# A transformer layer on one core: attention's weighted values issued four steps at a time, with two score banks and four maximum banks

## The chip, the cores and the metric

The kernel runs on one core of a Trainium2 chip. The metric is the time of one launch on the device in microseconds (us); the median of three runs is compared. The engines of the core are TensorE (PE, with its weight loads listed apart as PEld), VectorE (DVE), ScalarE (ACT), GpSimd (POOL) and SyncE (SP), which here only issues DMAs. They run side by side, each through its own list of instructions in order, and wait for one another on semaphores.

## What is computed

A layer with modulated layer norms: attention, then a feed-forward stage. The change lies in the attention, which is, for 4 sequences of 2048 tokens, 512 channels and 16 heads of 32:

```python
k = (c_kv @ W_k_up).reshape(Bb, Tt, NH, HD)
v = (c_kv @ W_v_up).reshape(Bb, Tt, NH, HD)
q = (x @ W_q).reshape(Bb, Tt, NH, HD)
scores = jnp.einsum('bqhd,bkhd->bhqk', q, k)
scores = scores + jnp.einsum('bqr,bkr->bqk', q_rope, k_rope)[:, None]
scores = jnp.where(causal[None, None], -jnp.inf, scores / scale)
w = jax.nn.softmax(scores, axis=-1)
attn = jnp.einsum('bhqk,bkhd->bqhd', w, v).reshape(Bb, Tt, D_MODEL)
```

All is in float32. Projections before it and the feed-forward stage behind it are not touched.

## The kernel before

Three stages follow one another: `projection`, `attention`, `feedforward`. The attention works in 16 **units** u (4 sequences by 4 groups of `GH` = 4 heads). A unit has 4 chunks j of 512 queries. Chunk j needs 4(j+1) **steps** i, each a block of 128 keys against the chunk's queries; a unit has 40 steps s, chunk 0 the steps 0 to 3, chunk 1 the steps 4 to 11, chunk 2 the steps 12 to 23 and chunk 3 the steps 24 to 39. The last four steps of a chunk are on the diagonal, and only 512, 384, 256 and 128 queries wide (`step_width`).

- **Scores** (`scores`, lines 1206 and 1207): for each of the four heads of a step two matmuls into one bank of PSUM, out of `SBANKS` = 3 that are used in turn. ScalarE takes the exponential of a head (line 1046) into a buffer of probabilities, `RING` = 5 of them. The first matmul of a head waits until ScalarE is through with the head that used the bank before (`probs_ready`, at + 1).
- **Weighted values** (`weighted_values`, lines 1213 and 1231): probabilities times values into the bank `ps_o`, 32 output columns for each head. They come `LAG` = 2 steps late and two steps at a time, in a **part** behind the scores of every odd step (`over_two_steps`).
- **Denominators**: the sums over keys. `SHARE_OF` gives each step an owner. Probabilities of a step "G" are added up by POOL (lines 1143 and 1146), those of a step "T" go through TensorE against ones into the bank `ps_d`. `close_denominators` (line 1245) puts POOL's sum into `ps_d` once for each chunk, in the part that takes the chunk's last steps. VectorE then inverts `ps_d` in four instructions (line 1095) and multiplies (line 1099); the list `extras` puts these among the maxima of the two steps behind the part.
- **Maxima** (`maximum`, line 1190): the row maxima that the exponentials subtract are worked out ahead for the next unit, in 160 **pieces** a unit (one matmul each, into one of `MBANKS` = 3 banks), reduced by VectorE (line 1082 for whole blocks, 1085 for those on the diagonal, whose widths are 128 to 512). `deal` spreads the pieces over the steps by a price list: `streams(m)` is TensorE's time in a pair of steps, `closes(m)` what VectorE's closing work takes from the pair at `FIRST[j] + 2`, the steps 2, 6, 14 and 26. TensorE issues pieces between the heads of a step and behind its part (the loop at line 1264).
- **Low queries**: `q_b`, `QB_RING` = 3 buffers, loaded by SP (`load_q_b`) in the order written in `body`; a row of each takes the negated maxima (`place_max`).

The loop that sets TensorE's order:

```python
for t in range(NU * NSTEP + LAG):
    parts = [lambda hh=hh: scores(*STEP_OF[t], hh) for hh in range(GH) if t < NU * NSTEP]
    closing = CLOSE_AT.get(t)
    if t > LAG and t % 2 == 1:
        parts.append(lambda: over_two_steps(t, closing))
    items = PLAN.get(t, [])
    for n, part in enumerate(parts):
        part()
        for it in items[len(items) * n // len(parts):len(items) * (n + 1) // len(parts)]:
            maximum(it)
```

## Time and profile before

| what | value |
|---|---|
| median of 3 runs | 3611.91 us (3610.14 to 3612.38) |
| the profiled execution | 3614.76 us, its span 3613.0 us |
| granted TensorE clock, mean | 0.990 |
| TensorE matmuls busy | 3506.1 us (97%) |
| VectorE busy | 2540.1 us (70%) |
| GpSimd busy | 2673.6 us (74%) |
| ScalarE busy | 1811.9 us (50%) |

A share is busy time over the whole span. A matmul's end is modelled and matmuls overlap, so a share of 97% does not say that each moment did work: how far TensorE runs at its pace is read from the distance between the starts of its rows.

### The profile page before, as it was taken

The numbers are of one execution on the slowest core, as the hardware profiler recorded it, in microseconds if no ns is written. First come the engines' busy times: TensorE is split into PE (matmuls) and PEld (weight loads), VectorE is DVE, ScalarE is ACT, GpSimd is POOL, SyncE is SP. The second block draws the span as 40 slices with busy tenths as digits, with TensorE's granted clock in tenths as the row PEclk, the third lists the DMA queues.
The fourth block names the chain that finished last, engine by engine and source line by source line (L and its number), as shares of the span: only waits on it lengthen the run. The fifth ranks groups of instructions, "written<-read, shape, count | busy, mean of one in ns | idle before, by whom it ended". The sixth has DMA issues, their size and how long they took to land. (4 is left out here: it accounts for less than half of the span.)

```text
span 3613.0 us, 54217 instructions
## 1 busy us (share of the span) xinstructions
PE 3506.1 (97%) x19552; PEld 2408.8 (67%) x19552; DVE 2540.1 (70%) x5329; ACT 1811.9 (50%) x3455; POOL 2673.6 (74%) x1194
## 2 busy tenths in 40 slices
PE   8999989999999999999999999999999699999999
PEld 4777756666666666666666666666665488888887
DVE  6676777777777777677777777777775366666665
ACT  2434335555555555555555555555555344444443
POOL 2333349889898898898988989889889566666665
PEclk9999989999999999999999999999999799999999
DMA  5778763463534535436346353463552111212120
GB/s 197 272 273 304 260 169 72 108 140 78 132 87 110 138 79 117 113 90 146 80 100 147 74 131 92 102 138 83 114 125 72 62 59 70 70 70 71 70 70 36
DMA packets 232756, 426.58 MB, mean 118 GB/s; under 512 B 25380, under 2 KB 26916, under 8 KB 232488
## 3 DMA queue, kind: packets, MB, share of 16 engines
q1 hardware_dynamic: 232424, 423.10, 43.2%
q8 instruction: 155, 2.54, 0.3%
q14 instruction: 113, 0.93, 0.1%
q10 hardware_dynamic: 64, 0.02, 0.0%
HBM read 300.86 MB, written 121.65 MB: 117 GB/s over the span
## 5 line engine op out<-in xcount | busy, mean ns | idle before, releaser
L1046 ACT ACTIVATE att_probs<-att_ps_s 128x512 f32<-128x512 f32 (+3 forms) x2560 | 1301.7, 536 | 938.7 <-PE att_ps_s L1207 850.1
L1146 POOL TENSOR_TENSOR att_sum_g<-att_sum_g,att_probs 128x2048 f32<-128x2048 f32 (+3 forms) x400 | 1626.0, 4065 | 72.8 <-ACT att_probs L1046 34.0
L1082 DVE TENSOR_REDUCE att_piece_max<-att_ps_m 128x1 f32<-128x512 f32 x1520 | 945.5, 681 | 136.1 <-PE att_ps_m L1190 134.2
L1206 PE MATMUL att_ps_s<-att_q_a,att_k_a 128*128 128x512 f32 (+3 forms) x2560 | 952.0, 374 | 17.2 <-DMA att_q_b<-att_neg_max 7.0
L1207 PE MATMUL att_ps_s<-att_q_b,att_k_b 65*128 65x512 f32 (+3 forms) x2560 | 934.6, 367 | 0.0
L1085 DVE CUSTOM_DVE_ANT_0 att_ps_m<-att_ps_m,mask_qk 128x128 f32<-128x128 f32 x1008 | 477.6, 508 | 268.2 <-PE att_ps_m L1190 254.9
L1190 PE MATMUL att_ps_m<-att_k_a,att_q_a 128*128 128x512 f32 (+3 forms) x1808 | 650.6, 384 | 5.9 <-DVE att_piece_max L1085 3.6
L1206 PEld LDWEIGHTS att_ps_s<-att_q_a,att_k_a 128*128 128x128 f32 x2560 | 486.1, 190 | 129.6 <-ACT att_probs L1046 42.5
L1213 PE MATMUL att_ps_o<-att_probs,att_v 128*32 128x512 f32 (+3 forms) x5120 | 546.8, 536 | 4.2 <-POOL att_probs L1126 4.2
L1207 PEld LDWEIGHTS att_ps_s<-att_q_b,att_k_b 65*128 65x128 f32 x2560 | 484.8, 189 | 65.7
L1190 PEld LDWEIGHTS att_ps_m<-att_k_a,att_q_a 128*128 128x128 f32 x1808 | 341.2, 190 | 225.0 <-issue 76.2
L1095 DVE RECIPROCAL att_ps_d<-att_ps_d 128x128 f32<-128x128 f32 x256 | 235.3, 943 | 156.4 <-PE att_ps_d L1213 156.4
L1143 POOL TENSOR_TENSOR att_sum_g<-att_probs 128x1536 f32<-128x1536 f32 (+1 forms) x64 | 275.8, 4310 | 87.1 <-ACT att_probs L1046 85.8
L1213 PEld LDWEIGHTS att_ps_o<-att_probs,att_v 128*32 128x32 f32 x5120 | 139.0, 109 | 279.9 <-issue 204.9
L1126 POOL TENSOR_SCALAR_AFFINE_SELECT att_probs<-att_probs 128x512 f32<-128x512 f32 x256 | 160.5, 640 | 142.0 <-ACT att_probs L1046 141.8
L1190 PE MATMUL att_ps_m<-att_k_next,att_q_a 128*128 128x128 f32 (+1 forms) x720 | 255.6, 388 | 0.0
L1190 PEld LDWEIGHTS att_ps_m<-att_k_next,att_q_a 128*128 128x128 f32 x720 | 131.4, 189 | 87.8 <-DVE att_piece_max L1082 27.4
L513 POOL TENSOR_TENSOR prj_h_lo<-prj_h_f,prj_h_hi 128x512 fp32r<-128x512 f32 x64 | 84.2, 1342 | 112.4 <-ACT prj_h_hi L450 112.4
L1401 DVE TENSOR_TENSOR ffn_x<-ffn_ps_ffn,ffn_gate 128x512 f32<-128x512 f32 x64 | 44.2, 691 | 173.2 <-PE ffn_ps_ffn L62 173.2
L1562 ACT ACTIVATE ffn_act_f<-ffn_relu 128x512 f32<-128x512 f32 x64 | 40.5, 633 | 248.7 <-DVE ffn_relu L1474 248.6
L1085 DVE DVE_READ_ACCUMULATOR2_ANT att_piece_max<- 128x1 f32 x1008 | 143.5, 142 | 0.0
L1537 ACT CAST att_q_a<-ffn_ps_t 128x512 fp32r<-128x512 f32 x128 | 75.2, 588 | 128.5 <-DVE ffn_ps_t L1442 127.5
(189 smaller groups left out, 4955.8 us busy)
## 6 DMA issues: line engine op xcount, KB each, us to landing
att_q_a<-s_q_hi SPq DMA_DIRECT2D x128, 256.0 KB, 5.9
att_q_a<-s_qr_hi SPq DMA_DIRECT2D x128, 256.0 KB, 6.7
prj_x_sb<-in_x_dram SPq DMA_DIRECT2D x16, 1024.0 KB, 5.2
s_q_hi<-prj_q_hi SPq DMA_DIRECT2D x16, 1024.0 KB, 4.2
s_q_lo<-prj_q_lo SPq DMA_DIRECT2D x16, 1024.0 KB, 6.0
s_k_hi<-prj_k_hi SPq DMA_DIRECT2D x16, 1024.0 KB, 4.5
s_k_lo<-prj_k_lo SPq DMA_DIRECT2D x16, 1024.0 KB, 6.4
s_v<-prj_v_sb SPq DMA_DIRECT2D x16, 1024.0 KB, 9.1
```

The source lines that it names most:

```text
L513: pool.tensor_tensor(h[1][:, c, :], h_f[:, c, :], as_f32(h[0][:, c, :]), ALU.subtract).then_inc(hlo_ready, 1)
L1046: act.activation(probs[t % RING][:, hh, c0:CH], ps_s[(GH * t + hh) % SBANKS][:, c0:CH], ACT.Exp, scale=SCALE).then_inc(probs_ready, 1)
L1082: dve.tensor_reduce(top, ps_m[:, bank, :], AX_X, ALU.max).then_inc(piece_taken, 1)
L1085: dve.tensor_tensor_reduce(ps_m[:, bank, 0:width], ps_m[:, bank, 0:width], keep["mask_qk"][:, CH - width:CH], 1.0, MASKED, ALU.add, ALU.ma ...
L1095: dve.reciprocal(cols, cols).then_inc(rden_ready, 1)
L1126: pool.affine_select(out=at, in_=at, compare_op=ALU.is_ge, fill=0.0, base=0, pattern=[[0, GH], [1, P]], channel_multiplier=-1).then_inc(cl ...
L1143: pool.tensor_tensor(sum_g[:, :, c0:CH], first[:, :, c0:CH], new, ALU.add).then_inc(sum_added, 1)
L1146: pool.tensor_tensor(sum_g[:, :, c0:CH], sum_g[:, :, c0:CH], new, ALU.add).then_inc(sum_added, 1)
L1190: mm(ps_m[:, bank, 0:width], q_a[j][:, hh, r * P:(r + 1) * P], keys, start=True, stop=True).then_inc(piece_ready, 1)
L1206: mm(out[:, c0:CH], k_a[:, hh, i * P:(i + 1) * P], q_a[j][:, hh, c0:CH], start=True, stop=False)
L1207: last = mm(out[:, c0:CH], k_b[:, hh, i * P:(i + 1) * P], q_b[low_queries(u, j)][0:2 * HD + 1, hh, c0:CH], start=False, stop=True)
L1213: last = mm(out[hh * HD:(hh + 1) * HD, c0:CH], stat(hh), mov[:, hh, c0:CH], start=start, stop=stop, skip_group_check=True)
```

## The change

Eight edits, all in the attention. The weighted values of four steps go in one part, behind every fourth step (`TOGETHER` = 4), not of two behind every second. The closings of chunks 1 and 2 come one part later, four steps on (`CLOSE_LATER`), and in every part the closing stands behind the values; the copy of `ps_o` by ScalarE stays where it was (`TAKE_AT`). There are six probability buffers, not five, two buffers of low queries, not three, two score banks, not three, and four maximum banks, not three. SP loads the low queries later and in another order. `deal` counts the values of four steps at the pair that holds them, at most `VALUES_MOST` = 9 for a pair, and shifts pieces by up to a step; its `closes` still names the steps 2, 6, 14 and 26.

```diff
-RING = 5
-QB_RING = 3
-SBANKS = 3
-MBANKS = 3
+RING = 6
+TOGETHER = 4
+QB_RING = 2
+SBANKS = 2
+MBANKS = 4
...
-ENDS_ON_PE = [owners[-1] == "T" for owners in SHARE_OF]
-OPENED_BY_SUM = ["T" not in owners.rstrip("T") for owners in SHARE_OF]
+CLOSE_LATER = (0, 4, 4, 0)
+OPENED_BY_SUM = ["T" not in owners for owners in SHARE_OF]
...
-    due = [(2 * m - 2) % NSTEP, (2 * m - 1) % NSTEP]
+    due = [(2 * m - n) % NSTEP for n in range(1, TOGETHER + 1)] if 2 * m % TOGETHER == 0 else []
...
-    return own / CH + GH * any(FIRST[j] == (2 * m) % NSTEP for j in range(TCH))
+    return (own + min(values, VALUES_MOST * CH)) / CH
+VALUES_MOST = 9
 PIECE, CLOSING = 2.8, 19
...
-            out[2 * m + half] = items[done:round(seen)]
+            some = items[done:round(seen)]
+            for n, it in enumerate(some):
+                at = 2 * m + half + (n + 0.5) / len(some) - 2 * pairs[0]
+                out.setdefault(2 * pairs[0] + int(at * pace), []).append(it)
...
-        CLOSE_AT = {NSTEP * u + FIRST[j] + STEPS[j] - 1 + LAG: (u, j) for u in range(NU) for j in range(TCH)}
+        TAKE_AT = {NSTEP * u + FIRST[j] + STEPS[j] - 1 + LAG: (u, j) for u in range(NU) for j in range(TCH)}
+        CLOSE_AT = {t + CLOSE_LATER[j]: (u, j) for t, (u, j) in TAKE_AT.items()}
...
                     wait_alone(sp, scores_ready, GH * (NSTEP * u + NSTEP), sp_mark)
                     place_max(u + 1, 1)
+                    load_q_b(u + 1, 1)
                     load_k_a(u + 1, TCH - 1)
                     load_q_a(u + 1, TCH - 1)
-                    load_q_b(u + 1, 2)
                     load_k_b(u + 1, TCH - 1)
...
-            def over_two_steps(t, closing):
-
-                if closing and ENDS_ON_PE[closing[1]]:
-                    close_denominators(*closing)
-                for due in (t - LAG - 1, t - LAG):
+            def over_four_steps(t, closing):
+
+                for due in range(t - LAG - TOGETHER + 1, t - LAG + 1):
                     weighted_values(*STEP_OF[due])
-                if closing and not ENDS_ON_PE[closing[1]]:
+                if closing:
                     close_denominators(*closing)
...
-                if t > LAG and t % 2 == 1:
-                    parts.append(lambda: over_two_steps(t, closing))
+                if t > LAG and (t - LAG) % TOGETHER == TOGETHER - 1:
+                    parts.append(lambda: over_four_steps(t, closing))
```

How many pieces stand in each step of a middle unit follows from `maximum_plan`, steps 0 to 39 (turns of a finished set of maxima are counted with them):

```
before 6 0 0 6 6 1 1 5 5 3 3 5 6 0 1 5 6 5 6 5 5 1 0 6 5 1 0 6 6 6 5 7 6 6 5 5 6 4 4 5
now    7 3 0 4 6 3 1 4 7 3 1 5 7 2 0 6 6 5 5 6 6 1 0 0 7 6 0 1 7 7 5 4 7 6 4 6 6 5 2 3
```

TensorE's instructions from the start of step 27 of unit 8, before: `att_ps_s2`, `s0`, `s1` are the score banks, two matmuls a head, `att_ps_m` takes a piece.

```order
L1206 MATMUL att_ps_s2<-att_q_a3,att_k_a 128x512
L1207 MATMUL att_ps_s2<-att_q_b2,att_k_b 128x512
L1190 MATMUL att_ps_m<-att_k_next,att_q_a0 128x128
L1206 MATMUL att_ps_s0<-att_q_a3,att_k_a 128x512
L1207 MATMUL att_ps_s0<-att_q_b2,att_k_b 128x512
L1190 MATMUL att_ps_m<-att_k_next,att_q_a0 128x256
L1206 MATMUL att_ps_s1<-att_q_a3,att_k_a 128x512
L1207 MATMUL att_ps_s1<-att_q_b2,att_k_b 128x512
L1190 MATMUL att_ps_m<-att_k_next,att_q_a0 128x384
```

The same place now (line 1212 is what was 1206, 1213 was 1207, 1196 was 1190):

```order
L1212 MATMUL att_ps_s0<-att_q_a3,att_k_a 128x512
L1213 MATMUL att_ps_s0<-att_q_b1,att_k_b 128x512
L1212 MATMUL att_ps_s1<-att_q_a3,att_k_a 128x512
L1213 MATMUL att_ps_s1<-att_q_b1,att_k_b 128x512
L1212 MATMUL att_ps_s0<-att_q_a3,att_k_a 128x512
L1213 MATMUL att_ps_s0<-att_q_b1,att_k_b 128x512
L1212 MATMUL att_ps_s1<-att_q_a3,att_k_a 128x512
L1213 MATMUL att_ps_s1<-att_q_b1,att_k_b 128x512
L1196 MATMUL att_ps_m<-att_k_next,att_q_a0 128x256
```

The heads follow one another with no piece between, and the third of them needs the bank of the first; before, a piece stood behind each head, and the fourth head needed the bank of the first.

VectorE's instructions around the closing of chunk 1 in a middle unit, before: the reciprocals are the inversions, `att_o_sb` the multiplication, the others reduce pieces.

```order
L1095 RECIPROCAL att_ps_d<-att_ps_d 128x128 x2
L1082 TENSOR_REDUCE att_piece_max<-att_ps_m 128x1 x2
L1095 RECIPROCAL att_ps_d<-att_ps_d 128x128
L1082 TENSOR_REDUCE att_piece_max<-att_ps_m 128x1
L1095 RECIPROCAL att_ps_d<-att_ps_d 128x128
L1082 TENSOR_REDUCE att_piece_max<-att_ps_m 128x1
L1099 TENSOR_TENSOR att_o_sb<-att_o_sb,att_ps_d 128x512
```

And now, from the first reciprocal of that closing:

```order
L1101 RECIPROCAL att_ps_d<-att_ps_d 128x128
L1091 ISA att_ps_m,att_piece_max<-att_ps_m,mask_qk 128x128
L1091 ISA att_piece_max 128x1
L1091 ISA att_ps_m,att_piece_max<-att_ps_m,mask_qk 128x256
L1091 ISA att_piece_max 128x1
L1101 RECIPROCAL att_ps_d<-att_ps_d 128x128
L1091 ISA att_ps_m,att_piece_max<-att_ps_m,mask_qk 128x384
L1091 ISA att_piece_max 128x1
L1091 ISA att_ps_m,att_piece_max<-att_ps_m,mask_qk 128x512
```

The inversions moved from the steps 14 and 15, which hold 1 and 5 pieces before, to the steps 18 and 19, which now hold 5 and 6.

## Rows read from the trace of the kernel before

**Rows 1.** the page's busy times, slices of the span and granted clock

```profile
PE 3506.1 (97%) x19552; PEld 2408.8 (67%) x19552; DVE 2540.1 (70%) x5329; ACT 1811.9 (50%) x3455; POOL 2673.6 (74%) x1194
...
PE   8999989999999999999999999999999699999999
...
PEclk9999989999999999999999999999999799999999
```

**Rows 2.** windows: the first unit, units 7 and 8, the last; busy us, count

```profile
473.46:645.56 172.10, 163.12 (x910) 103.29 (x911) 130.96 (x313) 84.94 (x163) 131.24 (x47) 0.96 0.44 98
1524.20:1670.46 146.26, 144.61 (x893) 92.28 (x894) 108.44 (x252) 83.82 (x164) 128.88 (x47) 1.00 0.47 109
1670.46:1816.66 146.20, 144.53 (x893) 92.36 (x894) 108.45 (x252) 83.86 (x164) 128.84 (x47) 1.00 0.47 109
2694.13:2823.65 129.52, 126.51 (x778) 75.56 (x779) 62.40 (x136) 77.51 (x159) 113.00 (x40) 0.99 0.27 78
```

**Rows 3.** timeline of PE, entry and exit of a part; start, us

```profile
1401.06 0.40 PE L1207 MATMUL att_ps_s<-att_q_b,att_k_b 65*128 65x512 f32 x1
1401.29 0.39 PE L1190 MATMUL att_ps_m<-att_k_a,att_q_a 128*128 128x512 f32 x1
1401.61 1.92 PE L1213 MATMUL att_ps_o<-att_probs,att_v 128*32 128x512 f32 x16
1403.46 0.50 PE L1190 MATMUL att_ps_m<-att_k_a,att_q_a 128*128 128x512 f32 x1
1403.80 0.39 PE L1206 MATMUL att_ps_s<-att_q_a,att_k_a 128*128 128x512 f32 x1
```

**Rows 4.** timeline of PE, the part that closes a chunk

```profile
1422.07 0.86 PE L1213 MATMUL att_ps_o<-att_probs,att_v 128*32 128x256 f32 x16
1423.61 1.07 PE L1213 MATMUL att_ps_d<-att_sum_g,ones 128*32 128x512 f32 x8 [0.68 <-POOL att_sum_g L1146]
1424.60 0.50 PE L1206 MATMUL att_ps_s<-att_q_a,att_k_a 128*128 128x512 f32 x1
```

**Rows 5.** waits: engine and line, releaser, us in total, times, longest

```profile
PE att_ps_d L1213 <- POOL att_sum_g L1146: 24.4, 31, 2.7
```

**Rows 6.** timeline, heads of step 26 of unit 8, no maximum between

```profile
1761.36 0.39 PE L1206 MATMUL att_ps_s<-att_q_a,att_k_a 128*128 128x512 f32 x1
...
1762.03 4.32 ACT L1046 ACTIVATE att_probs<-att_ps_s 128x512 f32<-128x512 f32 x8 [0.28 <-PE att_ps_s L1207]
...
1762.68 0.19 PEld L1206 LDWEIGHTS att_ps_s<-att_q_a,att_k_a 128*128 128x128 f32 x1 [0.18 <-ACT att_probs L1046]
1762.77 0.41 PE L1206 MATMUL att_ps_s<-att_q_a,att_k_a 128*128 128x512 f32 x1
```

**Rows 7.** timeline, heads of step 22, 256 wide

```profile
1747.89 0.36 PE L1206 MATMUL att_ps_s<-att_q_a,att_k_a 128*128 128x256 f32 x1
...
1748.85 0.19 PEld L1206 LDWEIGHTS att_ps_s<-att_q_a,att_k_a 128*128 128x128 f32 x1 [0.20 <-ACT att_probs L1046]
1748.85 0.39 PE L1206 MATMUL att_ps_s<-att_q_a,att_k_a 128*128 128x256 f32 x1
```

**Rows 8.** groups of VectorE's instructions in unit 7

```profile
L1082 DVE TENSOR_REDUCE att_piece_max<-att_ps_m 128x1 f32<-128x512 f32 x96 | 59.7, 681 | 8.0 <-PE att_ps_m L1190 7.9
L1085 DVE CUSTOM_DVE_ANT_0 att_ps_m<-att_ps_m,mask_qk 128x128 f32<-128x128 f32 (+1 forms) x64 | 30.3, 508 | 17.2 <-PE att_ps_m L1190 16.3
L1095 DVE RECIPROCAL att_ps_d<-att_ps_d 128x128 f32<-128x128 f32 x16 | 14.7, 943 | 6.0 <-PE att_ps_d L1213 6.0
...
L1099 DVE TENSOR_TENSOR att_o_sb<-att_o_sb,att_ps_d 128x512 f32<-128x512 f32 x4 | 2.7, 676 | 0.0
```

**Rows 9.** DMA issues by line, KB each, us to landing

```profile
att_q_b<-s_qr_lo SPq DMA_DIRECT2D x64, 256.0 KB, 8.1
...
att_k_next<-s_kr_lo SPq DMA_DIRECT2D x15, 256.0 KB, 6.5
```

**Rows 10.** POOL's full-width addition, whole span

```profile
L1146 POOL TENSOR_TENSOR att_sum_g<-att_sum_g,att_probs 128x2048 f32<-128x2048 f32 x288 | 1323.7, 4596 | 64.4 <-ACT att_probs L1046 34.0 <-POOL att_sum_g L1146 0.4
```

More of the change, by code:

```diff
@@ L715, in streams, with deal @@
     own = sum(2 * GH * step_width(s) for s in (2 * m, 2 * m + 1))
-    due = [(2 * m - 2) % NSTEP, (2 * m - 1) % NSTEP]
+    due = [(2 * m - n) % NSTEP for n in range(1, TOGETHER + 1)] if 2 * m % TOGETHER == 0 else []
+    values = 0
     for s in due:
         j = max(j for j in range(TCH) if FIRST[j] <= s)
-        own += GH * step_width(s) * (2 if SHARE_OF[j][s - FIRST[j]] == "T" else 1)
-    return own / CH + GH * any(FIRST[j] == (2 * m) % NSTEP for j in range(TCH))
+        values += GH * step_width(s) * (2 if SHARE_OF[j][s - FIRST[j]] == "T" else 1)
+    return (own + min(values, VALUES_MOST * CH)) / CH
+VALUES_MOST = 9
 PIECE, CLOSING = 2.8, 19
-def deal(items, pairs):
+def deal(items, pairs, pace):
     closes = lambda m: CLOSING * any(FIRST[j] + 2 == 2 * m for j in range(TCH))
@@ L756, in maximum_plan @@
         for items, pairs in spans:
-            for t, some in deal(items, pairs).items():
-                plan[t - 1 if u else t] += some
+            for t, some in deal(items, pairs, 1 - 1 / NSTEP if u else 1).items():
+                plan[t] += some
     for t in range(NU * NSTEP - 1, -1, -1):
@@ L766, in low_queries @@
 def low_queries(u, j):
-    return 1 if (u, j) == (NU - 1, TCH - 1) else (TCH * u + j) % QB_RING
+    return j % QB_RING
 def operands(nc, ctx):
@@ L957, in load_for_last_stage @@
                     load_weight(0)
-                    load_weight(3)
                 else:
                     load_weight(j)
+                    if j == 2:
+                        load_weight(3)
             def body(u, nxt):
@@ L967, in body @@
                     wait_alone(sp, scores_ready, GH * (NSTEP * u + STEPS[0]), sp_mark)
+                    load_q_b(u, 2)
                     load_q_a(u + 1, 0)
-                    load_q_b(u, 3)
                 else:
+                    wait_alone(sp, scores_ready, GH * (NSTEP * u + STEPS[0]), sp_mark)
+                    load_q_b(u, 2)
                     load_for_last_stage(0)
@@ L975, in body @@
                     wait_alone(sp, scores_ready, GH * (NSTEP * u + FIRST[1] + STEPS[1]), sp_mark)
+                    load_q_b(u, 3)
                     load_q_a(u + 1, 1)
-                    load_q_b(u + 1, 0)
                 else:
@@ L1061, in _ @@
                     place_first_max(1)
-                if t in CLOSE_AT:
-                    take_output(*CLOSE_AT[t])
+                if t in TAKE_AT:
+                    take_output(*TAKE_AT[t])
         @block.vector
@@ L1132, in add @@
                 c0 = CH - step_width(s)
-                new = probs[s % RING][:, :, c0:CH]
+                new = probs[(NSTEP * u + s) % RING][:, :, c0:CH]
                 if i >= TB * j:
@@ L1138, in add @@
                 if i == mine[1]:
-                    first = probs[(FIRST[j] + mine[0]) % RING]
+                    first = probs[(NSTEP * u + FIRST[j] + mine[0]) % RING]
                     pool.wait_ge(closed, max(1, TCH * u + j))
@@ L1230, in weighted_values @@
                     pe.wait_ge(v_in[j], 16 * u + 16)
-                last = over_keys(ps_o, lambda hh: v[:, i // TB, i % TB, hh * HD:(hh + 1) * HD], probs[s % RING],
+                last = over_keys(ps_o, lambda hh: v[:, i // TB, i % TB, hh * HD:(hh + 1) * HD], probs[(NSTEP * u + s) % RING],
                                  start=(i == 0), stop=(i == STEPS[j] - 1), c0=c0)
@@ L1236, in weighted_values @@
                         pe.wait_ge(o_ready, TCH * u + j + 1)
-                    last = over_keys(ps_d, ones, probs[s % RING], start=first, stop=(i == STEPS[j] - 1), c0=c0)
+                    last = over_keys(ps_d, ones, probs[(NSTEP * u + s) % RING], start=first, stop=False, c0=c0)
                 last.then_inc(pv_done, 1)
@@ L1244, in close_denominators @@
                 pe.wait_ge(sum_added, summed(u, j, SHARE_OF[j].rindex("G")))
-                last = over_keys(ps_d, ones, sums[j % 2], start=opens, stop=not ENDS_ON_PE[j])
+                last = over_keys(ps_d, ones, sums[j % 2], start=opens, stop=True)
                 last.then_inc(closed, 1)
-            def over_two_steps(t, closing):
-                if closing and ENDS_ON_PE[closing[1]]:
-                    close_denominators(*closing)
-                for due in (t - LAG - 1, t - LAG):
+            def over_four_steps(t, closing):
+                for due in range(t - LAG - TOGETHER + 1, t - LAG + 1):
                     weighted_values(*STEP_OF[due])
-                if closing and not ENDS_ON_PE[closing[1]]:
+                if closing:
                     close_denominators(*closing)
```

7 lines of the change are left out of this document (2 added, 5 removed).

## The prediction, made before the changed kernel was run

> **What bounds the kernel now.** I read the page first: TensorE is busy 97% of the span at full clock, the others much less [rows 1]. That share is modelled, so I went on to the windows: a middle unit takes 146.2 us each time, the first 172.1, the last, which has few maxima to work out, 129.5 [rows 2]. The reader should see there that POOL does 128.9 us of work in the 146.2, VectorE 108.4 and ScalarE 83.8: none of them is the bound, but POOL is near it. Then I read the timeline of TensorE and took distances between starts. A matmul 512 wide follows the next after 0.23 us (1401.06 to 1401.29) [rows 3]; widths of 384, 256 and 128 take in proportion, 0.18, 0.12 and 0.06 to 0.11. Eight 32-column matmuls of 512 (one step of values, or one closing) take 0.86 us: a part of sixteen lasts 1.85 (1401.61 to 1403.46) and one of eight 0.99 (1423.61 to 1424.60), and their difference is 0.86 [rows 3, 4].
>
> With these prices a middle unit's work adds up: 272 widths of 512 in the scores (28 full steps of 8 matmuls, and 48 for the twelve narrow ones) and 136 in the 160 pieces (96 whole, 64 of a mean 320) are 408 times 0.2325, or 94.9; values of 34 full steps' worth, denominators of 4.25 and four closings are 42.25 times 0.86, or 36.3. That is 131.2 of the 146.2. The rest: 20 parts at 0.33 (below) are 6.6, waits of closings for POOL's sum 1.6, waits for score banks 1.1, and 5.7 that no row names singly, narrow matmuls whose weight loads (0.19) outlast them and pieces behind the inversions.
>
> **What is taken away.** A part costs more than its matmuls: 0.09 on entry (1401.29 to 1401.61 is 0.32, not 0.23), 0.13 inside (0.99 against 0.86), and 0.11 behind it (1403.46 to 1403.80 is 0.34) [rows 3, 4]. That is 0.33 each time TensorE changes between matmuls of 128 and of 32 columns. Ten parts fewer in a unit are **-3.3 us**. The Trainium skill's page TensorEngine Tiling (Array Packing), section Key Properties, says that a change of tiling mode drains the array; the trace agrees with 0.33 us, and by that rule alone the change would only gain.
>
> Closings wait for POOL's sum 24.4 us in all [rows 5], 1.6 a unit, 0.87 of it where chunk 1 closes: its values are through by 1422.72 (0.65 us for widths 256 and 128), and the closing starts at 1423.61 [rows 4]. Behind its values, and for chunks 1 and 2 four steps on, POOL has 3 us or more to spare: **-1.6 us**. Together -4.9 a unit.
>
> **What is added: the second bank to wait for.** A head's first matmul waits for the exponential of the head that had its bank. Step 26 of unit 8 shows what that takes, since no piece stands between its heads: the first starts at 1761.36, ScalarE starts on it at 1762.03, and the weight load of the fourth, which wants its bank, is let go at 1762.68 and the matmul starts at 1762.77 [rows 6]. So a head can follow the one before it in its bank no sooner than 1.41 us. With three banks the three heads between take 3 times 0.465, 1.395: all but nothing is lost. With two banks there are two heads between, 0.93 us, and the pair is short by 0.48, unless pieces fill it at 0.23 each; two whole pieces do. At width 256 the same cycle is 0.96 (1747.89 to 1748.85) [rows 7]; I take 1.2 at 384 and 0.75 at 128, estimates between and below these two.
>
> I counted the pairs of heads in a middle unit by the pieces that stand with them, leaving out the last pair ahead of each part, which the part covers. Of 44 pairs in full steps 8 have no piece (3.8 us) and 2 have one (0.7); the others have two to four, but pieces on the diagonal are narrow, so 1.3 us is lost there too. The 20 pairs in narrow steps lose 5.6, nearly all in steps 2, 10, 22 and 23 and at 9, 21 and 38. The sum is 11.3. Before, the same count with three banks gives 1.1: **+10.2 us**. The bounds: if the cycle were 0.1 shorter 7, if it were 0.1 longer 15. In the last unit 28 pairs have no piece, and the sum is 20.9 against 2.2. The Trainium skill's page Perfetto Trace Analysis, section Identifying Performance Opportunities, says that a gap which repeats on the engine that should be saturated can mean too few PSUM buffers for the next tile. By it this edit is the one to fear, and the trace agrees so far as rows 6 go: three banks are just enough, short by 0.015 us.
>
> **What is moved: VectorE's closing work.** Four inversions at 0.92 and a multiplication at 0.68 are 4.4 us; a whole piece is 0.62, one on the diagonal some 0.46 (unit 7's 108.4 busy us less 59.7, 14.7, 2.7 and 1.9 for small ones, over 64) [rows 2, 8]. For chunks 1 and 2 this work now falls in steps 18 and 19, and 30 and 31, whereas `closes` still keeps 14 and 26 free. Steps 30 to 32 hold 16 whole pieces: VectorE needs 9.9 + 4.4 = 14.3, TensorE 9.4 with its bank waits. Four banks let it be four pieces, 2.5 us, ahead, so it waits 2.4. Steps 18 to 20 hold 17, nearly all diagonal: 12.3 against 8.6, less 1.8, a wait of 1.9. Steps 2 to 4 give 0.9. Of this 5.2 I set off 1.6 that such waits take before (they lie in the 5.7): I take **+3 us**, with 0 and 6 as ends, since 0 is what a fourth bank gives if VectorE catches up in the bank waits, and 6 what the whole 5.2 and some more at 24, 28 and 36 come to.
>
> **What costs nothing.** Six buffers, not five, keep ScalarE's place: buffer t-6 is given back by the first step of the part, long before step t+1 has scores; POOL's additions of 4.6 us [rows 10] get one step more of slack, and if POOL were late it would be by under 1. The low queries of chunk 1 are now loaded only at a unit's end, with four steps left, 14 us in the new order. SP issues two loads behind the row of maxima and nothing else; such loads land after 6.5 us when last of four, 8.1 when last of six [rows 9]. So 4 us or more are left; without that cover each unit would wait a few us at step 4. The other loads have 8 steps or more.
>
> **The sum.** Middle unit: -3.3 - 1.6 + 10.2 + 3 = +8.3 us. The first is alike (its pairs lose 11.5). The last: -4.9 + 18.7 + 0.5 = +14.3. 15 times 8.3 and 14.3 are +139. The profiled execution takes 3614.8, so 3754; the median of the runs shown lies 2.9 below it: **3751 us**, 3.8% slower.
>
> **The rivals.** *The score banks do not bind, and it is faster.* For it speaks that ScalarE is half idle and takes eight in 4.32, one each 0.54, when it has work [rows 6]: it is no bound in throughput. Against it, that what counts is the delay of one head, and the row has it. If no wait came (and none on VectorE), 16 times -4.9 and the 1.1 now lost give some 3515; with VectorE's 3 us, 3563. The cycle would have to be below 1.11 us for the change to gain with that term, 1.2 without it; 1.41 stands in the row, made of 0.67 from the head's start to ScalarE's, 0.65 from there to the weight load and 0.09 to the matmul, and no part of it depends on how many banks there are. I give it 8 in 100.
> *The terms cancel*: a cycle of 1.2 and nothing on VectorE, 3612, 3 in 100.
> *VectorE becomes the bound.* The inversions hold up the pieces, the late pieces leave heads without filling, and both waits add rather than cover one another: 6 for VectorE and 15 for the banks is +15 a unit, 3855. For it speaks that in steps 28 to 33, parts left out, it needs 7 us more than TensorE; against it that most parts then give it 3.5 us or more to catch up. 8 in 100.
> *Merged parts do not save*, since each step in them waits anew for its buffer: the sixteen matmuls of two steps go through without a gap [rows 3], so I see no reason; it would add 16 times 3.3 and give 3804, within the range.
> The forecast's case keeps 81 in 100.
>
> **The numbers.** The range goes from +4 a unit (7 for the banks, 1.5 for VectorE) to +12 (12 and 5): 3680 to 3810, rounded. A difference of 0.2%, 7 us, is what the measurement can tell. Faster 0.08, same 0.03, slower 0.89.
>
> **What would show it.** The profile after should have units of some 154 to 155 us; waits of PE's weight load at the scores for the exponentials several times those before, 0.4 to 0.5 us each, at steps 14, 22, 23, 26 and 27, of which the full ones take 2.8 us each. No wait of closings for POOL. Maxima that wait for VectorE in steps 18 to 20 and 30 to 33. Parts of four full steps that last 3.6 us. If units take under 146 us, the cycle is not 1.41 with two banks, and I am wrong there; if steps 0 to 3 end late by a load, in the queue.

## The result, and the profile after

The changed kernel takes 3933.6 us (median of 4 runs, 3931.2 to 3935.5) against 3612.1 us: the ratio is 1.089, its 95% interval 1.087 to 1.091. The direction was forecast, the size was not: +321 us where the prediction has +139, and the time lies 124 us above its range. The page of the profile after, busy time by engine, TensorE's slices and its granted clock by slice:

```profile
span 3929.5 us, 54201 instructions
...
PE 3667.3 (93%) x19552; PEld 2436.4 (62%) x19552; DVE 2519.2 (64%) x5329; ACT 1837.7 (47%) x3455; POOL 2671.8 (68%) x1194
...
PE   8999899999999999898999999989999979999999
...
PEclk9999999999999999999999999999999989999999
```

The counts are those of [rows 1], and VectorE, ScalarE and POOL do the same work in the same time. TensorE's busy time rose by 161 us for the same 19552 matmuls (ends are modelled, and a matmul at half clock counts for longer), and idle time by 155 (span less busy, 262 against 107). The mean granted clock fell from 0.990 to 0.971. There are two levels, 1.2 and 2.4 GHz, so 0.971 is 2 x 0.029 x 3929.5 = 228 us at the lower one, against 72 before: at most half of the difference, 78 us, can be due to the clock.

The windows of a middle unit, of its steps 26, 32, 33 and 34, and of step 24 of the next unit. The columns are the stretch and its length, busy time and count of PE, PEld, DVE, ACT and POOL, granted clock, DMA share, GB/s:

```profile
1834.00:1999.11 165.11, 153.69 (x894) 92.97 (x892) 107.00 (x253) 85.33 (x165) 128.81 (x46) 0.98 0.42 96
1936.09:1938.89 2.80, 2.40 (x11) 1.22 (x9) 1.01 (x4) 2.07 (x5) 1.81 (x1) 1.00 0.00 0
1959.50:1965.79 6.29, 4.87 (x16) 2.50 (x15) 6.29 (x11) 2.88 (x5) 4.55 (x1) 1.00 0.29 92
1965.79:1978.52 12.73, 8.09 (x55) 3.59 (x54) 5.08 (x9) 2.47 (x5) 9.12 (x2) 0.91 1.06 241
1978.52:1983.06 4.54, 4.54 (x14) 3.69 (x14) 2.14 (x8) 1.79 (x3) 0.00 (x0) 0.51 0.33 72
2091.43:2096.00 4.57, 4.57 (x16) 3.87 (x16) 2.37 (x10) 2.11 (x5) 4.07 (x2) 0.63 0.79 189
```

Units that took 146.2 take 165 to 169 (mean of the middle ones 167), the first 192.2 instead of 172.1, and the last, up to the start of its step 39, 152.4 instead of 129.5 [rows 2]. But the last unit doesn't end there. In the kernel before, TensorE then stood for ScalarE and POOL:

```profile
2827.29 0.38 PE L1206 MATMUL att_ps_s<-att_q_a,att_k_a 128*128 128x128 f32 x1 [2.57 <-ACT att_probs L1046]
...
2832.13 1.93 PE L1213 MATMUL att_ps_o<-att_probs,att_v 128*32 128x512 f32 x8 [4.24 <-POOL att_probs L1126]
...
2839.73 1.07 PE L1213 MATMUL att_ps_d<-att_sum_g,ones 128*32 128x512 f32 x8 [2.68 <-POOL att_sum_g L1146]
```

In the changed kernel one wait of 1.53 us for POOL is left there. From its first score to the end of its last matmul the unit takes 148.0 us before and 159.9 now, so 12 us of the loss lie in it, 20 in the first unit and some 286 in the fourteen between. To see where, I took the length of each of the 40 steps, from its first matmul of scores to that of the next step, as a median over thirteen middle units (all "steps" below are such medians; their sum is 146.2 before and 167.0 after). Four steps stand out. Step 33, which holds a part, takes 13.17 us; the same part and pieces take 7.8 where nothing holds them. Step 34 takes 4.58 and, in most units, step 24 takes 4.55, at clocks of 0.51 and 0.63, though TensorE is busy all through both. Step 32 takes 6.28 where its matmuls need 3.5 (15 full-width ones at 0.2325).

What ended TensorE's waits, with us in total, times, longest:

```profile
PEld att_ps_s L1212 <- ACT att_probs L1052: 266.8, 817, 1.0
...
PEld att_ps_m L1196 <- DVE att_piece_max L1088: 112.2, 231, 1.2
...
PE att_ps_m L1196 <- DMA att_k_a<-s_kr_lo: 76.8, 15, 6.3
PEld att_ps_m L1196 <- DVE att_piece_max L1091: 68.4, 126, 0.9
...
PE att_ps_d L1219 <- POOL att_sum_g L1152: 1.5, 1, 1.5
```

The first, second and fourth are the waits that the prediction speaks of, for score banks and for VectorE. In the kernel before, the first was:

```profile
PEld att_ps_s L1206 <- ACT att_probs L1046: 42.5, 204, 2.7
```

A weight load (PEld) can wait while a matmul still runs (at 1937.46, in step 26, the load had waited 0.65 us and its matmul 0.21), so not all of these 266.8 us are lost; the matmuls themselves (PE) wait 48.2 us for exponentials. The last row answers to [rows 5]: of 24.4 us of waiting for POOL 1.5 are left. The third was not foreseen: once in each of the fifteen units before the last, a piece waits for its keys. The timeline of TensorE there:

```profile
1972.16 1.04 PE L1219 MATMUL att_ps_o<-att_probs,att_v 128*32 128x512 f32 x8
1973.13 0.50 PE L1196 MATMUL att_ps_m<-att_k_next,att_q_a 128*128 128x512 f32 x1
1978.28 0.44 PE L1196 MATMUL att_ps_m<-att_k_a,att_q_a 128*128 128x128 f32 x1 [4.64 <-DMA att_k_a<-s_kr_lo]
1978.52 0.74 PE L1212 MATMUL att_ps_s<-att_q_a,att_k_a 128*128 128x512 f32 x1
1979.06 0.63 PE L1213 MATMUL att_ps_s<-att_q_b,att_k_b 65*128 65x512 f32 x1
1979.49 0.41 PE L1196 MATMUL att_ps_m<-att_k_a,att_q_a 128*128 128x256 f32 x1
```

Behind the part TensorE stands for 4.64 us, and then it runs at half clock for 4.5 us: matmuls 512 wide follow each other after 0.43 us (1979.06 to 1979.49), not 0.23 [rows 3]. Who is late is read from VectorE's timeline and from that of SP's queue in the same unit:

```profile
1959.52 0.96 DVE L1101 RECIPROCAL att_ps_d<-att_ps_d 128x128 f32<-128x128 f32 x1
...
1962.33 0.67 DVE L1105 TENSOR_TENSOR att_o_sb<-att_o_sb,att_ps_d 128x512 f32<-128x512 f32 x1
```

```profile
1928.59 0.43 SPq L820 DMA_DIRECT2D att_q_a<-s_qr_hi  x1
1963.10 0.34 SPq L949 DMA_DIRECT2D s_o<-att_o_sb  x1
...
1967.20 0.30 SPq L831 DMA_DIRECT2D att_k_a<-s_k_hi  x1
...
1968.49 0.43 SPq L831 DMA_DIRECT2D att_k_a<-s_kr_lo  x1
```

Chunk 2 is closed four steps later, behind step 29; its outputs are ready at 1963.0. In SP's fixed order their store (`store_o(u, 2)`, line 996) stands ahead of the next unit's keys, so SP stands 34 us, and the keys of two chunks, four loads to `k_a` and two to `k_b` for each, are issued behind it in one go. Those of chunk 1, at 1967.20 to 1968.49, could have gone at 1959.5, when the scores of step 31 were through. The pieces want them at 1973.6 and get them at 1978.28.

### The profile page after: what moved, and what is told of

The parts are those of the page before. It is cut to its first block and busy times, and to the rows that moved or that the text cites. A ratio compares the mean times of both kernels' runs of the same rounds, so it can differ in the third digit from the quotient of the medians.

```text
span 3929.5 us, 54201 instructions
## 1 busy us (share of the span) xinstructions
PE 3667.3 (93%) x19552; PEld 2436.4 (62%) x19552; DVE 2519.2 (64%) x5329; ACT 1837.7 (47%) x3455; POOL 2671.8 (68%) x1194
## 5 line engine op out<-in xcount | busy, mean ns | idle before, releaser
L1052 ACT ACTIVATE att_probs<-att_ps_s 128x512 f32<-128x512 f32 (+3 forms) x2560 | 1326.7, 533 | 1159.5 <-PE att_ps_s L1213 1013.3
L1212 PE MATMUL att_ps_s<-att_q_a,att_k_a 128*128 128x512 f32 (+3 forms) x2560 | 1030.5, 406 | 70.7 <-ACT att_probs L1052 48.2
L1213 PE MATMUL att_ps_s<-att_q_b,att_k_b 65*128 65x512 f32 (+3 forms) x2560 | 961.1, 377 | 0.0
L1196 PE MATMUL att_ps_m<-att_k_a,att_q_a 128*128 128x512 f32 (+3 forms) x1808 | 660.1, 391 | 113.8 <-DMA att_k_a<-s_kr_lo 76.8
L1212 PEld LDWEIGHTS att_ps_s<-att_q_a,att_k_a 128*128 128x128 f32 x2560 | 497.6, 194 | 338.4 <-ACT att_probs L1052 266.8
L1196 PEld LDWEIGHTS att_ps_m<-att_k_a,att_q_a 128*128 128x128 f32 x1808 | 353.5, 196 | 312.6 <-issue 138.0
L1213 PEld LDWEIGHTS att_ps_s<-att_q_b,att_k_b 65*128 65x128 f32 x2560 | 500.6, 196 | 42.2
L1219 PE MATMUL att_ps_o<-att_probs,att_v 128*32 128x512 f32 (+3 forms) x5120 | 513.5, 532 | 0.0
L1219 PEld LDWEIGHTS att_ps_o<-att_probs,att_v 128*32 128x32 f32 x5120 | 150.1, 110 | 298.3 <-issue 245.6
L1196 PE MATMUL att_ps_m<-att_k_next,att_q_a 128*128 128x128 f32 (+1 forms) x720 | 266.0, 403 | 21.2 <-DVE att_piece_max L1088 20.0
L1196 PEld LDWEIGHTS att_ps_m<-att_k_next,att_q_a 128*128 128x128 f32 x720 | 143.4, 201 | 118.0 <-DVE att_piece_max L1088 61.0
```

Of the source, the lines that this page charges most:

```text
L1052: act.activation(probs[t % RING][:, hh, c0:CH], ps_s[(GH * t + hh) % SBANKS][:, c0:CH], ACT.Exp, scale=SCALE).then_inc(probs_ready, 1)
L1196: mm(ps_m[:, bank, 0:width], q_a[j][:, hh, r * P:(r + 1) * P], keys, start=True, stop=True).then_inc(piece_ready, 1)
L1212: mm(out[:, c0:CH], k_a[:, hh, i * P:(i + 1) * P], q_a[j][:, hh, c0:CH], start=True, stop=False)
L1213: last = mm(out[:, c0:CH], k_b[:, hh, i * P:(i + 1) * P], q_b[low_queries(u, j)][0:2 * HD + 1, hh, c0:CH], start=False, stop=True)
L1219: last = mm(out[hh * HD:(hh + 1) * HD, c0:CH], stat(hh), mov[:, hh, c0:CH], start=start, stop=stop, skip_group_check=True)
```

## The experiments

The first four each change one thing in the changed kernel. Theory A was that this late store is the largest new loss (7 us and more a unit), and that the prediction's own terms make up the rest; theory B that the score banks do, and that the late keys only cover bank waits.

**store_late.** The store moves behind the loads of the next unit's first two chunks of keys.

```diff
                 else:
                     load_for_last_stage(2)
-                store_o(u, 2)
+                    store_o(u, 2)
...
                         if c == 1:
+                            store_o(u, 2)
                             place_max(u + 1, 0)
```

> The changed kernel, with the store of chunk 2's output moved in SP's list from ahead of the next unit's key loads to behind the second of them. Theory A (the later closing holds up SP's queue, the keys of chunk 1 come late, TensorE stands at step 33 for some 5 us and then works at half clock for a while): step 33 falls from 13 to under 8 us and step 34 from 4.5 to 3, some 7 us a unit for 15 units, 3830 us. Theory B (these stalls only sit where VectorE or the score banks would hold TensorE anyway): 3900 us or more.

Measured 3823.3 us, 1.058 [1.056, 1.059], so 110 us less than the changed kernel. Windows of a unit, of its step 33 and step 34:

```profile
1772.02:1931.79 159.77, 152.95 (x893) 92.48 (x892) 106.77 (x253) 85.40 (x165) 128.87 (x46) 0.99 0.44 100
1905.25:1912.98 7.73, 7.73 (x56) 3.48 (x54) 4.39 (x8) 2.47 (x5) 7.43 (x2) 1.00 0.21 43
1912.98:1915.78 2.80, 2.80 (x14) 1.99 (x12) 2.38 (x8) 1.78 (x3) 1.73 (x1) 1.00 0.65 180
```

Step 33 falls from 13.17 to 7.76 and step 34 from 4.58 to 2.79, no other step by more than 0.1: the wait for keys is worth 5.4 us a unit (the trace has 76.8 over fifteen, 5.1) and the half clock behind it 1.8. The late keys are shown, a third of the loss.

**close_at_once.** `-CLOSE_LATER = (0, 4, 4, 0)`, `+CLOSE_LATER = (0, 0, 0, 0)`: the closings go back to their own part; all else stays.

> The changed kernel with the closings of chunks 1 and 2 back in the part that takes their last steps (CLOSE_LATER all 0). Theory A: the stand at step 33 goes (5 us and 1.6 for the clock), VectorE's inversions fall where the deal of the pieces keeps room for them (3 to 4 us at steps 19, 20 and 32), and the wait for POOL's sum returns (1.6): 9 us a unit less, 3795 us. Theory B (bank waits are the loss): no more than 3 us a unit less, 3885 us.

Measured 3768.5 us, 1.043 [1.041, 1.045]: 165 us less. Step 33 falls as above, and steps 20 and 32 fall from 4.41 and 6.28 to 3.02 and 3.53. These two hold what VectorE's inversions cost in the wrong place; where the closing of chunk 1 is back, step 16 rises from 3.27 to 4.98. The expected return of the wait for POOL did not come:

```profile
PE att_ps_d L1219 <- POOL att_sum_g L1152: 1.7, 1, 1.7
```

Behind the values of four steps the closings find POOL's sum ready in their own part. So moving them four steps on, which the late store and the misplaced inversions come from, gained nothing.

**banks33.** Three score banks and three maximum banks in the changed kernel.

```diff
-SBANKS = 2
-MBANKS = 4
+SBANKS = 3
+MBANKS = 3
```

> The changed kernel with three score banks and three maximum banks, all else as changed. Theory A: bank waits of 10 to 11 us a unit go, and the stretch at half clock at step 24 (1.5 us) with them, 18 more in the last unit; the late keys stay: 3740 us. Theory B (bank waits make up nearly the whole loss of 21 us a unit): 3620 us or less.

Measured 3872.3 us, 1.071 [1.069, 1.073]: both theories missed, the gain is 61 us. The last unit, which has few pieces, gets to its step 39 18 us sooner (134 us, not 152), but 12 of them are lost again in waits for POOL, and to its last matmul it is 6 us shorter (153.9 against 159.9). In a middle unit ten steps with narrow heads or few pieces (2, 6, 10, 14, 22 to 24, 26, 27 and 38) get shorter by 6.8 us together, two thirds of what the forecast had for the banks; but step 4 rises from 3.92 to 6.35, and steps 5, 8, 12 and 28 by 0.3 to 0.7. TensorE's waits for VectorE show why:

```profile
PEld att_ps_m L1196 <- DVE att_piece_max L1088: 184.3, 378, 1.5
PEld att_ps_m L1196 <- DVE att_piece_max L1091: 115.1, 243, 1.0
```

They were 112.2 and 68.4: with VectorE's work in bursts, giving up the fourth maximum bank takes back about half of what the third score bank gives. Part of that is the clock, and the units of this run show how much. Steps 4 and 5 of one unit, then of the next:

```profile
1488.36:1493.36 5.00, 3.54 (x16) 2.24 (x14) 4.92 (x16) 1.83 (x4) 3.98 (x2) 1.00 1.05 254
1493.36:1499.89 6.53, 6.53 (x68) 3.63 (x68) 2.47 (x11) 3.33 (x6) 3.57 (x1) 1.00 1.05 222
1651.19:1657.55 6.36, 4.89 (x16) 3.35 (x15) 5.35 (x18) 1.99 (x4) 3.98 (x2) 0.71 0.79 199
1657.55:1665.50 7.95, 7.95 (x68) 4.75 (x68) 2.31 (x9) 3.35 (x6) 3.59 (x1) 0.80 1.06 229
```

The order is the same, and in both TensorE waits four times for VectorE, 1.6 us in all; the second unit is at half clock for part of the way and takes 2.8 us longer. Of the fifteen units behind the first, eight are like the second of these and six like the first; one has the half clock in step 5 alone.

**deal_moved.** The planner keeps free the pairs in which the closing work now falls.

```diff
-    closes = lambda m: CLOSING * any(FIRST[j] + 2 == 2 * m for j in range(TCH))
+    closes = lambda m: CLOSING * any(FIRST[j] + 2 + CLOSE_LATER[j - 1] == 2 * m for j in range(TCH))
```

> The changed kernel with the deal's closes() moved to the steps where the inversions now fall (18 and 30 in place of 14 and 26). Theory A: VectorE's hold on TensorE at steps 19, 20 and 32 shrinks by 3 to 4 us a unit, and steps 14 and 26 get pieces between their heads, which saves 1 to 1.5 us of bank waits: 3860 us. If the late keys cover step 32's wait, half of it: 3895 us.

Measured 3847.6 us, 1.065 [1.063, 1.067]: 86 less. Step 32 falls from 6.28 to 3.60, step 19 from 3.67 to 2.93, and steps 33 and 20 by 0.5 and 0.3: together 4.3 us a unit for a table entry that still named the old steps.

The next five were made to part what stays.

**before24.** The kernel before with `SBANKS = 2` and `MBANKS = 4`, nothing else.

> The kernel before with two score banks and four maximum banks and nothing else changed: the price of the banks by itself. Theory A (a head can follow the one before it in its bank no sooner than 1.41 us): the pairs of heads of the old deal come short by 10.9 us a unit and 18.9 in the last, less 1.1 and 2.2 before, and the fourth maximum bank gives back some 1.5: 3614 + 15 x 8.3 + 15, 3755 us. Theory B (the banks are not where the time went): under 3680 us.

Measured 3711.1 us, 1.028 [1.026, 1.029]: 98 slower, less than expected. Its waits for the exponentials, and the window of step 26:

```profile
PEld att_ps_s L1206 <- ACT att_probs L1046: 276.0, 947, 0.7
```

```profile
1810.20:1812.94 2.74, 2.31 (x9) 1.16 (x7) 2.39 (x4) 2.12 (x5) 2.74 (x1) 1.00 0.00 0
```

A middle unit gets longer by 6.3 us, not 10.2, and the last, up to its step 39, by 13 (129.5 to 142.5), not 18.7; to its last matmul only by 6 (148.0 to 154.2), since TensorE stood for POOL there before. Step 26 is as forecast, 2.74 against 1.89; but steps 3, 11 and 39, in which the count had waits too, stay or get shorter by up to 0.4: the waits for score banks take the place of others there, and the fourth maximum bank, I take it, gives some back.

**close0_33.** The changed kernel with three and three banks and the closings at once: of the change, the parts of four steps, the closing behind the values, the new deal, the six buffers and the two buffers of low queries are left.

> The changed kernel with three score and three maximum banks and all closings in the part that takes a chunk's last steps: what is left is the values of four steps in one part, the sixth probability buffer, two buffers of low queries and the deal. Theory A now (a part of 3.6 us leaves VectorE without pieces when its three banks are read, and it lacks that time in the steps between): slower than before by 7 us a unit, 3725 us. Theory B (the merge saves its 3.3 us a unit once the banks and closings are as they were): 3560 to 3590 us.

Measured 3724.5 us, 1.031 [1.029, 1.032]: this remainder, called the merged parts from here on, is 112 us slower. Of 40 steps in windows of four (one merged part each), three hold the loss: steps 2 to 5 take 17.4 us against 13.3 before, 6 to 9 16.2 against 14.4, 14 to 17 17.7 against 15.7; the others together are 0.6 shorter. Steps 4 and 5 of a unit:

```profile
1889.69:1896.06 6.37, 4.91 (x16) 3.35 (x15) 5.37 (x18) 1.99 (x4) 3.98 (x2) 0.71 1.02 250
1896.06:1903.96 7.90, 7.90 (x69) 4.71 (x68) 2.31 (x9) 3.31 (x6) 3.58 (x1) 0.80 1.06 217
```

The three windows follow the closings in steps 1, 5 and 13; behind the one in step 25 nothing is lost and nothing gained. VectorE is busy 5.37 of the 6.37 us of step 4. Its timeline there, and TensorE's:

```profile
1890.03 0.37 DVE L1091 CUSTOM_DVE_ANT_0 att_ps_m<-att_ps_m,mask_qk 128x256 f32<-128x256 f32 x1
...
1890.32 0.96 DVE L1101 RECIPROCAL att_ps_d<-att_ps_d 128x128 f32<-128x128 f32 x1
```

```profile
1893.01 0.69 PE L1196 MATMUL att_ps_m<-att_k_a,att_q_a 128*128 128x384 f32 x1 [0.82 <-DVE att_piece_max L1091]
1893.49 0.63 PE L1212 MATMUL att_ps_s<-att_q_a,att_k_a 128*128 128x512 f32 x1
```

An inversion of 0.96 stands between every two pieces of 0.4, so each piece behind them waits for its bank, up to 0.82 us; and then TensorE falls to half clock, into step 5, which doesn't wait at all. All units from the third on have this; by the pair of units under banks33 the clock is, as an estimate, 2.8 of the 7.3 us that a middle unit loses here. POOL is waited for 1.3 us in all, so this order also has the 1.6 us a unit that its closings no longer wait.

**late_and_moved.** store_late and deal_moved together.

> The changed kernel with both repairs, the store of chunk 2's output behind the key loads, and the deal's closes() at the steps of the inversions. Theory A: the two losses lie at different steps and add up, 110 and 66 us less than 3931: 3757 us. If moving pieces hits the late keys or the banks elsewhere, only the larger: 3820 us.

Measured 3749.6 us, 1.038 [1.037, 1.040]: 184 less than the changed kernel, where the two alone add up to 196. Its clock is 0.989; the half clock in step 24 is still there in seven units. What stays of the loss is 137 us.

**behind.** The kernel before, with only the part of the change that the trace spoke for: the closing behind the values in every part, chunk 1's one part (two steps) later, and the planner told of it.

```diff
-ENDS_ON_PE = [owners[-1] == "T" for owners in SHARE_OF]
+CLOSE_LATER = (0, 2, 0, 0)
+ENDS_ON_PE = [False for owners in SHARE_OF]
...
-    closes = lambda m: CLOSING * any(FIRST[j] + 2 == 2 * m for j in range(TCH))
+    closes = lambda m: CLOSING * any(FIRST[j] + 2 + CLOSE_LATER[j - 1] == 2 * m for j in range(TCH))
```

> The kernel before (parts of two steps, three and three banks) with two things alone: every closing stands behind the values of its part, and that of chunk 1 comes one part, two steps, later, with closes() moved along. Theory A (the closings' wait for POOL, 1.6 us a unit, is real time of TensorE and goes, and VectorE finds its place): 3590 us. Theory B (POOL's wait only covers another wait): 3610 to 3620 us.

Measured 3589.5 us, 0.9935 [0.992, 0.995]: 23 us faster than the kernel before, and the best of all. A unit, and its steps 13 and 25, in which a chunk's values end:

```profile
1658.90:1803.80 144.90, 144.66 (x894) 92.12 (x894) 108.67 (x252) 83.95 (x164) 128.85 (x47) 1.00 0.48 110
1702.31:1706.34 4.03, 4.03 (x30) 2.79 (x29) 3.80 (x7) 2.92 (x6) 3.78 (x3) 1.00 0.59 127
1743.97:1748.38 4.41, 4.40 (x43) 2.34 (x43) 1.01 (x4) 3.15 (x6) 4.26 (x3) 1.00 0.53 109
```

They took 4.49 and 4.96. The forecast's 1.6 us a unit for POOL was right: it is 1.4. The interval lies wholly below 1, so the gain is clear of noise, though it is under 1%.

Next came the question what the merged parts lose to. Theory A: VectorE's closing work in a burst with the pieces. Theory B: the parts themselves.

**before_small** and **merged_small.** In the kernel before, and in close0_33, the inversions take 8 of their 128 columns; 120 columns are left out of each, and VectorE's closing work shrinks from 4.4 to some 1.5 us.

```diff
-                cols = ps_d[:, r * P:(r + 1) * P]
+                cols = ps_d[:, r * P:r * P + 8]
```

> The kernel before, its four inversions of a closing over 8 of the 128 columns each, so that 120 columns are left out of each inversion and VectorE's closing work falls from 4.4 us to some 1.5. Control for the next run. Theory A: steps 3 and 4 lose the 1.1 us that VectorE costs there, 1 to 1.5 us a unit: 3595 us.

> The changed kernel with three and three banks and all closings in the part that takes a chunk's last steps, and the inversions over 8 of 128 columns as in the run before this. Theory A (what the merge costs is VectorE's closing work in the three windows of steps 2 to 5, 6 to 9 and 14 to 17, and the half clock that the stand brings): 8 to 10 us a unit less than with whole inversions, below its control by the merge's own saving of 2 to 3 us a unit: 3560 us. Theory B (the merge itself starves an engine, whatever VectorE has to do): over 3650 us.

Measured 3600.2 us, 0.997 [0.996, 0.998], and 3602.4, 0.998 [0.997, 0.999]. The closing work costs the kernel before 10 us and the merged one 122. Steps 4 and 5 of a unit of merged_small, and its waits for VectorE at whole pieces and for POOL:

```profile
1825.79:1829.11 3.32, 3.01 (x16) 2.34 (x14) 3.25 (x12) 2.00 (x5) 3.32 (x2) 1.00 1.06 213
1829.11:1835.63 6.52, 6.52 (x69) 3.62 (x68) 2.47 (x11) 3.32 (x6) 4.65 (x3) 1.00 1.06 252
```

```profile
PEld att_ps_m L1196 <- DVE att_piece_max L1088: 112.1, 310, 0.6
...
PE att_ps_d L1219 <- POOL att_sum_g L1152: 1.4, 1, 1.4
```

Steps 4 and 5 fall by 3.0 and 1.4, at full clock. Theory A's cause holds for the whole loss of close0_33, the half clock included, which goes with the waits. Its 3560 us was missed by 42: units of 145.65 (before_small) and 145.61 are equal, where ten changes of shape at 0.33 and the waits for POOL had been saved. From its first matmul to the first behind it, the parts of a unit take 37.7 us against 39.9; 1.35 of these 2.2 us are the waits for POOL, the rest is that one part of four full steps takes 3.57 where two of two took 1.85 each. On the other side, steps hold six or seven pieces, and VectorE takes 0.62 a piece: where a piece follows a piece, the distances exceed what the widths need by 3.8 us a unit against 1.0. That this is what eats the saving is argued here, not shown; the next but one run tries it.

**spread33.** close0_33 with the closing work counted half at each of two pairs.

```diff
-    closes = lambda m: CLOSING * any(FIRST[j] + 2 == 2 * m for j in range(TCH))
+    closes = lambda m: CLOSING / 2 * any(2 * m in (FIRST[j] + 2, FIRST[j] + 4) for j in range(TCH))
```

> The changed kernel with three and three banks and closings in the part of a chunk's last steps, and the deal's closes() halved and laid over the four steps behind a closing, not over the first two alone: 11, 13 and 15 pieces in the three windows where there were 13, 15 and 17. Theory A (two pieces fewer are 1.2 us of VectorE in each window, and the half clock at steps 4 and 5 goes): 5 us a unit less than 3725, 3650 us. Theory B (VectorE isn't the cause): 3725 us.

Measured 3679.2 us, 1.019 [1.017, 1.021], between the times of theories A and B, 3650 and 3725: 45 less than close0_33. Step 4 falls from 6.36 to 4.52, step 5 from 7.90 to 6.56, step 8 from 5.57 to 4.89; seven of the fifteen units behind the first still have the half clock in step 5.

**flat33.** spread33, with the values of a part counted half at each of two pairs, so that the steps that held six or seven pieces hold fewer.

```diff
-    due = [(2 * m - n) % NSTEP for n in range(1, TOGETHER + 1)] if 2 * m % TOGETHER == 0 else []
+    due = [(2 * (m + m % 2) - n) % NSTEP for n in range(1, TOGETHER + 1)]
...
-    return (own + min(values, VALUES_MOST * CH)) / CH
+    return (own + values / 2) / CH
```

> The run spread33 with one thing more: the deal counts the values of four steps half at each of the two pairs of steps ahead of them, not all at the pair that holds them, so that steps 0, 8, 12 and 24 have 3 to 6 pieces where they had 5 to 7. Theory A (what the merge should have saved is lost where seven pieces in a step come faster than VectorE's 0.62 us for each): steps 0, 8, 12 and 24 take 0.5 to 1 us less each, and the windows behind closings, which get fewer pieces too, some 2 us: 4 us a unit less than spread33, 3620 us, and with luck the merge's 3.3 us a unit show. Theory B (the merge has nothing to save beyond what merged_small shows): 3680 us.

Measured 3677.7 us, 1.018 [1.017, 1.019], the same as spread33: a miss. Steps 0, 8, 12 and 24 fall by 0.9, 1.4, 1.2 and 0.6, and the pieces cost as much where they went (steps 2, 6, 7, 14, 28, 31, 33, by 0.2 to 0.7 each).

**all33.** late_and_moved with three and three banks, to price the banks in the changed order.

> The run late_and_moved with three score and three maximum banks in place of two and four: the price of the banks in the changed order, with the late keys and the misplaced closings out of the way. Theory A (in the merged order the banks' waits lie largely where VectorE would hold TensorE with three maximum banks, as close0_33 and banks33 suggest): 3 us a unit and 18 us in the last less than 3750, 3690 to 3700 us. Theory B (the price is what before24 shows for the old order, 6.4 us a unit and 13 in the last): 3640 us.

Measured 3724.0 us, 1.031 [1.029, 1.032]. The banks are worth 26 us in all, where both theories expected more. Nearly all of it lies in the middle units, 1.8 each (153.3 on the mean against 155.1); by the medians it is 0.9, since seven units of late_and_moved have the half clock in step 24. The last unit reaches its step 39 11 us sooner, but waits 8.6 us for POOL behind it and ends no sooner (155.1 us, and 155.2 in late_and_moved). And in this order step 4 again goes from 3.9 to 6.4, at a granted clock of 0.71 (window 1889.83 to 1896.20). all33 and close0_33 take the same time, 3724 us: with the store and the deal mended, the later closing neither costs nor gains.

## Why the prediction was wrong in size

The loss of 321 us comes apart as 184 that late_and_moved takes away, 26 for the banks and 112 for the merged parts (the remainder that close0_33 has, not the merging by itself). That is one order of taking it apart: the losses cover one another, and the banks are worth 98 us alone (before24), 61 in the changed kernel and 26 at the end.

- **"What costs nothing" failed.** "The other loads have 8 steps or more" was said of low queries. I had looked at what SP issues ahead of those, and not at what the later closing of chunk 2 makes late in SP's order: its own store, and the key loads behind it. It cost 110 us, 7.2 a unit, of which 1.8 is half clock that the stand leaves behind. The later closing wasn't needed either: "and for chunks 1 and 2 four steps on" was to free TensorE of POOL, and behind the values alone the wait is gone (close_at_once).
- **VectorE's moved work was too small**: +3 us a unit with 0 and 6 as ends, measured 4.3 (deal_moved, in steps 19, 20, 32 and 33), within the ends. The wait of 2.4 forecast for steps 30 to 32 is 2.7 in step 32 alone. The place and the cause were right; how much of the 1.6 that I set off for waits of before was there to be set off, no run shows.
- **The score banks were too large** in the middle units: +10.2, measured 6.3 alone and 0.9 to 1.8 in the corrected order. The cycle behind it was right, 1.41 us: in step 26 of the changed kernel heads start at 1936.09, 1936.61, 1937.46, 1938.04 and 1938.89, so every second comes 1.37 to 1.43 behind the one that had its bank, and the step takes 2.80 as forecast. What failed is the count: the waits of 44 pairs were added up as if nothing else held TensorE at those steps. Where VectorE holds it, the bank wait is covered, and the fourth maximum bank gives something back; that this makes up the missing 4 us is argued from the runs with both numbers changed, since none changes one alone. In the last unit 18.7 was forecast and 13 measured up to step 39, but only 6 count: the 129.5 us of [rows 2] end at the start of step 39, and behind it TensorE stood for POOL, which takes up what comes later. The prediction has no term for that.
- **The merged parts were wrong in sign**: -3.3 us a unit, measured +7.3 (close0_33), and 0 with the closing work taken away. The 0.13 inside a part is saved (3.57 against twice 1.85), and on entry the excess falls from 1.7 to 0.7 us a unit; with the -1.6 for POOL, which these runs have too, the two terms were -4.9 and came out at +7.3. But parts of four steps leave steps without a part, which the deal fills with six or seven pieces, at 0.62 us of VectorE each; no term counts that, and none asks what becomes of the 4.4 us of inversions when the pieces beside them stand closer; with the inversions all but gone, 122 us go. The rival "merged parts do not save" had the missing saving, which merged_small shows, and neither the reason nor the loss.
- **POOL's waits were right**: -1.6, measured -1.4 (behind).
- **The clock was left out.** It fell to half in step 34 of all units but the last, in step 24 of ten, and in close0_33 in steps 4 and 5. By the sum under the page it is up to 78 of the 321 us. The same steps at full clock, in store_late and in the other units, price step 34 at 1.8 us in fifteen units and step 24 at 1.45 in ten, 42 us together. In late_and_moved the clock is back at 0.989: most of it went with the waits that led to it.
- **The rival "VectorE becomes the bound"**, at 3855 us, was nearest. Its mechanism, that waits on VectorE hold up the pieces, is what close0_33, deal_moved and merged_small show; that both waits add rather than cover one another is not.

What was wrong, in one sentence: I priced each edit by the row next to it, and the largest costs were made by two edits meeting, a late closing with a queue's order and a burst of pieces with the inversions. What stays open is how clock and waits divide in the steps in which no two units differ by the clock alone, and whether a deal by a finer price list would let the merged parts gain; flat33 and spread33 are two tries of many. Some parts of the change were not tried alone: parts of four steps under the old deal, six buffers, fewer low-query buffers, the shift of pieces within a pair and the pace.

## What to carry to other kernels

When a result is made later, go down each queue written in a fixed order and ask what stands behind its store, down to the last load; a store that waits 34 us holds back every load behind it. When small pieces of work are merged on the bounding engine, look at what the gaps between them gave to the second engine: here its total stayed and its waits grew, and a planner's price list must move with them. Add up waits on two engines only where they fall at different steps. Follow the last unit to its last instruction, since an engine that is not the bound before can be it there.

## What the runs showed of the hardware

Half clock came not only behind a stand. After TensorE stood for 4.64 us, matmuls ran at 1.2 GHz for 4.5 us. But it also fell in step 24 of ten of the fifteen units before the last of the changed kernel, where no wait of the matmuls before it in steps 22 and 23 was over 0.24 us; the timeline of steps 22 to 24:

```profile
2088.83 0.39 PE L1212 MATMUL att_ps_s<-att_q_a,att_k_a 128*128 128x256 f32 x1 [0.23 <-ACT att_probs L1052]
...
2089.81 0.33 PE L1212 MATMUL att_ps_s<-att_q_a,att_k_a 128*128 128x128 f32 x1 [0.20 <-ACT att_probs L1052]
...
2092.06 0.61 PE L1212 MATMUL att_ps_s<-att_q_a,att_k_a 128*128 128x512 f32 x1
2092.46 0.63 PE L1213 MATMUL att_ps_s<-att_q_b,att_k_b 65*128 65x512 f32 x1
```

Small and narrow heads with waits of 0.2 us lead up to it, and from 2092.06 full-width matmuls follow each other after 0.40 to 0.43 us until 2095.7. In banks33 and close0_33, with three score banks, steps 22 and 23 lose these waits (1.94 to 1.31 and 1.61 to 1.25 us), and step 24 takes 3.4 to 3.5 in the fourteen units between the first and the last, at full clock. Two banks and such heads are not enough for it: before24 has them in step 22 too, but a part in step 23, and its step 24 is at full clock. The Trainium skill's page TensorE: Matmul & The Clock Gate, section A second HAM failure mode: psum-queue depth-cycling, tells of such clock losses from frequent short idling between groups of matmuls that go through PSUM's banks in turn; it tells of bf16, and these runs agree in float32, with some 1.5 us in each unit that has it (4.57 against 3.11 for the same step). That it comes in ten units of fifteen with the same order in each, no run here explains.
